# Waits on masks and layer norms themselves, and each value waited for once

## What is computed

```python
x = x + 0.5 * ffn0(layernorm(x))          # low rank: U1, V1, gelu, U2, V2
x = x + attn0(layernorm(x))               # 16 heads of 8, causal softmax, inner layer norm
x = x + 0.5 * ffn0(layernorm(x))
x = x + 0.5 * moe(layernorm(x))           # shared expert + top 2 of 8 experts
x = x + attn1(layernorm(x))               # causal, weight (second-order Taylor of exp), 16 heads
x = x + 0.5 * moe(layernorm(x))
```

## Time and profile before

| | us |
|---|---|
| median of three timed runs | 1515.85 (1515.03 to 1517.44) |
| profiled execution, its own time | 1510.05 |
| its span, first to last instruction | 1508.2 |
| TensorE matmul busy | 1238.7 (82%) |
| VectorE busy | 1078.3 (71%) |
| ScalarE busy | 750.7 (50%) |
| GpSimd busy | 308.1 (20%) |
| mean granted TensorE clock | 0.945 |

### The profile page before, as it was taken

How to read it: one execution, slowest core, us unless ns; L and a number is a source line. 1 busy time by engine, 2 the same in 40 slices (tenths; PEclk the granted TensorE clock), 3 DMA queues, 4 the chain that set the end, 5 groups by cost and what they waited for, 6 DMA issues and landing times. The chain is left out here.

```text
span 1508.2 us, 27324 instructions
## 1 busy us (share of the span) xinstructions
PE 1238.7 (82%) x10040; PEld 686.2 (45%) x10064; DVE 1078.3 (71%) x3235; ACT 750.7 (50%) x1246; POOL 308.1 (20%) x807
## 2 busy tenths in 40 slices
PE   5698659987798887888789877898778888898886
PEld 2354235444443454434454344544455345553544
DVE  6985368667886678866778658876687767866756
ACT  3166336652466425664276533765337653454442
POOL 1024001331014200242002420133101331122220
PEclk9699669999999989999889998999989999999999
DMA  3100000100010000100001000010000100101000
GB/s 115 43 2 1 7 22 15 29 8 22 8 33 12 8 22 8 43 2 10 27 1 43 8 10 20 1 43 8 21 9 3 42 1 5 46 1 43 2 1 14
DMA packets 37205, 28.77 MB, mean 19 GB/s; under 512 B 7961, under 2 KB 36305, under 8 KB 37073
## 3 DMA queue, kind: packets, MB, share of 16 engines
q1 hardware_dynamic: 37072, 27.04, 6.7%
HBM read 5.90 MB, written 2.10 MB: 5 GB/s over the span
## 5 line engine op out<-in xcount | busy, mean ns | idle before, releaser
L772 ACT ACTIVATE left<-bank 128x512 f32<-128x512 f32 x280 | 159.8, 600 | 84.3 <-PE bank L1242 81.4
L962 DVE TENSOR_REDUCE left<-bank 128x4 f32<-128x512 f32 x280 | 184.5, 683 | 23.1 <-PE bank L1223 21.7
L814 ACT ACTIVATE right<-bank 128x512 f32<-128x512 f32 x280 | 158.4, 601 | 85.6 <-PE bank L1329 79.0
L1165 PE MATMUL bank<-right,pairs 128*128 128x512 f16 x588 | 160.9, 397 | 23.7 <-DVE right L1041 17.1
L1221 PE MATMUL bank<-left 128*128 128x512 f16 (+1 forms) x448 | 128.5, 336 | 59.8 <-DVE left L952 28.5
L1092 DVE TENSOR_SCALAR right<-right 128x1024 f32<-128x1024 f32 x168 | 105.5, 654 | 62.0 <-ACT right L814 61.4
L1062 DVE SCALAR_TENSOR_TENSOR right<-bank,right 128x128 f32<-128x128 f32 x448 | 126.1, 344 | 30.6 <-PE bank L1305 23.9
L1355 PE MATMUL bank<-right 128*32 128x256 f32 (+3 forms) x1792 | 133.1, 435 | 0.0
L1305 PE MATMUL bank<-ew,right 128*128 128x128 f32 x896 | 119.3, 278 | 9.8 <-ACT right L791 6.0
L1305 PEld LDWEIGHTS bank<-ew,right 128*128 128x128 f32 x896 | 113.4, 191 | 29.8 <-DVE right L1062 11.5
L684 POOL TENSOR_TENSOR spareB<-neghalf 1x1 f32<-1x1 f32 x192 | 47.7, 249 | 327.9 <-DVE right L1092 252.5
(11 more groups left out here) (280 smaller groups left out, 2287.4 us busy)
## 6 DMA issues: line engine op xcount, KB each, us to landing
right<-right SPq DMA_DIRECT2D x168, 64.0 KB, 2.1
left<-left SPq DMA_DIRECT2D x168, 32.0 KB, 1.9
left<-x_dram SPq DMA_DIRECT2D x7, 256.0 KB, 2.8
out_dram<-right SPq DMA_DIRECT2D x7, 256.0 KB, 2.3
left<-left SPq DMA_DIRECT2D x24, 64.0 KB, 2.1
right<-right SPq DMA_DIRECT2D x24, 32.0 KB, 1.9
wo<-wo_dram SPq DMA_DIRECT2D x1, 512.0 KB, 3.2
ew<-ew_dram SPq DMA_DIRECT2D x1, 512.0 KB, 4.6
```

Of the source, the lines that this page charges most:

```text
L772: act.activation(h.probs[:, g % 2, u * S:(u + 1) * S], ps[:, :], ACT.Exp).then_inc(h.act, 1)
L814: act.activation(h.wts[:, p % 2, u * S:(u + 1) * S], ps[:, :], ACT.Square, bias=1.0, scale=FEAT ** -0.5).then_inc(h.act, 1)
L962: dve.tensor_reduce(h.bmax[:, u * NT:(u + 1) * NT], ps[:, :].rearrange("p (b k) -> p b k", k=P), AX.X, ALU.max).then_inc(h.dve, 1)
L1165: done = mm(out, left, right, start=first, stop=last)
```

## The change

`wait_apart`, the additions and the semaphore `carried` go; the masks' wait stands ahead of the first mask. The memset of one element goes from `Chain.then`, so that bn_aggr, max and the search for indices carry the wait on VectorE's own semaphore. A class `Passed` stands between the program and ScalarE's, VectorE's and TensorE's waits: it keeps the highest value that the engine has waited for on each semaphore and leaves out a wait for a value not above it. All `wait_ge`, `full` and `fill` of these three engines go through it; GpSimd's and SyncE's don't. The order lists and `LOOP` stay. Cut to its core:

```diff
-    def then(self, ins, carrier=None):
+    def then(self, ins):
         self.n += 1
         ins.then_inc(self.sem, 1)
         self.eng.wait_ge(self.sem, self.it * self.per + self.n)
-        if carrier is not None:
-            carrier()
...
+        class Passed:
+            def __init__(self, eng):
+                self.eng, self.seen = eng, {}
+
+            def wait_ge(self, sem, value):
+                if self.seen.get(sem.name, 0) < value:
+                    self.seen[sem.name] = value
+                    self.eng.wait_ge(sem, value)
...
-            for h in streams.values():
-                pool.tensor_tensor(h.spare[:, :], neghalf[0:1, 0:1], neghalf[0:1, 0:1], ALU.add).then_inc(h.carried, 1)
...
-            def wait_apart(h, it, n, sem, value):
-                pool.wait_ge(h.carried, it * h.carriers + n + 1)
-                pool.wait_ge(sem, value)
-                pool.tensor_tensor(h.spare[:, :], neghalf[0:1, 0:1], neghalf[0:1, 0:1], ALU.add).then_inc(h.carried, 1)
...
                 if u in COMPLETE0:
-                    wait_apart(h, it, g * NC + list(COMPLETE0).index(u), h.act, drained(h, it, step, "s"))
+                    pool.wait_ge(h.act, drained(h, it, step, "s"))
...
                     k = p * NC + list(COMPLETE1).index(u)
-                    wait_apart(h, it, k, h.plus1, it * NPAIR * NC + k + 1)
+                    pool.wait_ge(h.plus1, it * NPAIR * NC + k + 1)
...
-            def carrier():
-                dve.memset(spare_dve[:, :], 0.0)
...
-                h.chain.then(last, carrier)
+                h.chain.then(last)
...
-                pe.wait_ge(h.rrows_ready, it * 2 + p // GP + 1)
-                ps = fill(pe, h, it, step, "r")
+                passed.wait_ge(h.rrows_ready, it * 2 + p // GP + 1)
+                ps = fill(passed, h, it, step, "r")
```

More of the change, by code:

```diff
@@ L444, in attention_stream @@
             new = h.region.take
-            h.T, h.per, h.lns, h.carriers = TA, PERA, 4, NC * NG
+            h.T, h.per, h.lns = TA, PERA, 4
             h.ring, h.pv = h.banks[0:3], h.banks[3]
@@ L475, in taylor_stream @@
             new = h.region.take
-            h.T, h.per, h.lns, h.carriers = TB, PERB, 3, NC * NPAIR
+            h.T, h.per, h.lns = TB, PERB, 3
             h.ring, h.num, h.dsums = h.banks[0:2], h.banks[2], h.banks[3]
@@ L722, in norm @@
             def norm(h, it, k, step):
-                ps = full(act, h, it, step, "lnT")
+                ps = full(passed, h, it, step, "lnT")
                 if h in (A1, A2) and k == 2:
@@ L739, in down0 @@
                 if n % 2 == 0:
-                    ps = full(act, h, it, step, "mix")
+                    ps = full(passed, h, it, step, "mix")
                     act.activation(h.mixed[:, :], ps[:, :], ACT.Copy).then_inc(h.act, 1)
@@ L745, in up0 @@
                     f = int(unit[2:])
-                    ps = full(act, h, it, step, unit)
+                    ps = full(passed, h, it, step, unit)
                     act.activation(h.hid0[:, f, :], ps[:, :], ACT.Gelu_apprx_tanh, bias=b1[:, f:f + 1],
@@ L761, in shift @@
             def shift(h, it, g, step):
-                ps = full(act, h, it, step, "mT")
+                ps = full(passed, h, it, step, "mT")
                 act.activation(h.offs[:, g, :], ps[0:GH, :], ACT.Copy, scale=-1.0 / OFF_UNIT).then_inc(h.act, 1)
@@ L780, in gate @@
             def gate(h, it, n, step):
-                ps = full(act, h, it, step, "gate")
+                ps = full(passed, h, it, step, "gate")
                 act.activation(h.sgm[:, n % NS, :], ps[:, :], ACT.Sigmoid, scale=1 / W_SCALE)\
@@ L904, in down0 @@
                         tables_once()
-                    full(dve, h, it, f"norm {(0, 3)[n // 2]}", "lnT")
+                    full(passed, h, it, f"norm {(0, 3)[n // 2]}", "lnT")
                     h.chain.then(dve.tensor_tensor(h.ln[:, :, :], h.x[:, :, :], b2h[:, :, :], ALU.add))
                     return
-                ps = full(dve, h, it, step, "y")
+                ps = full(passed, h, it, step, "y")
                 first = h is A1 and isinstance(it, int) and it == 0
@@ L960, in rowmax @@
                     h.chain.start(it, chained(FRONT))
-                ps = full(dve, h, it, step, "s")
+                ps = full(passed, h, it, step, "s")
                 dve.tensor_reduce(h.bmax[:, u * NT:(u + 1) * NT], ps[:, :].rearrange("p (b k) -> p b k", k=P),
@@ L1011, in route @@
                 c = h.chain
-                dve.wait_ge(h.act, drained(h, it, f"router {n}", "router"))
-                c.then(dve.tensor_tensor(h.sel[:, :, :], h.s8[:, :, :], rbias[:, :, :], ALU.add), carrier)
+                passed.wait_ge(h.act, drained(h, it, f"router {n}", "router"))
+                c.then(dve.tensor_tensor(h.sel[:, :, :], h.s8[:, :, :], rbias[:, :, :], ALU.add))
                 for t in range(NT):
                     last = dve.max(h.top[:, t, :], h.sel[:, t, :])
-                c.then(last, carrier)
+                c.then(last)
                 for t in range(NT):
@@ L1049, in expert @@
                 if e == 0:
-                    dve.wait_ge(h.moe_out, first + 1)
+                    passed.wait_ge(h.moe_out, first + 1)
                     dve.scalar_tensor_tensor(out=h.acc[:, :, :].rearrange("p t d -> p (t d)"), in0=h.num[:, :],
@@ L1264, in out0 @@
             def out0(h, it, n, step):
-                pe.wait_ge(h.act, drained(h, it, "norm 2", "lnT"))
-                ps = fill(pe, h, it, step, "y")
+                passed.wait_ge(h.act, drained(h, it, "norm 2", "lnT"))
+                ps = fill(passed, h, it, step, "y")
                 for t in range(NT):
@@ L1300, in expert @@
                 else:
-                    pe.wait_ge(h.moe_added, first + e)
-                pe.wait_ge(h.act, drained(h, it, *unit_of_expert(n, e)))
+                    passed.wait_ge(h.moe_added, first + e)
+                passed.wait_ge(h.act, drained(h, it, *unit_of_expert(n, e)))
                 ps = (h.dsums, h.num)[e % 2]
@@ L1349, in num @@
                 if p:
[L1350 removed]
+                    passed.wait_ge(h.num_read, it * NPAIR + p)
                 for kt in (0, 1, 3, 2):
@@ L1368, in out1 @@
                 some = OUT1_PAIRS[n]
-                ps = fill(pe, h, it, step, "y")
+                ps = fill(passed, h, it, step, "y")
                 for p in some:
-                    pe.wait_ge(h.dve, drained(h, it, f"scale {p}", "r"))
+                    passed.wait_ge(h.dve, drained(h, it, f"scale {p}", "r"))
                     for t in range(NT):
```

236 lines of the change are left out of this document (118 added, 118 removed).

## The result

The changed kernel takes 1499.62 us in the median of 7 runs (1498.10 to 1502.16), the kernel before, on the same chip and between them, 1515.85 us (7 runs, 1506.00 to 1517.44): a ratio of 0.9903, interval 0.9881 to 0.9926. The change does what it says and more than three times what its own steps were held to be worth.

The account below looks back on a forecast made before the run. Hand-overs between engines were taken to bound the kernel; 0.35 + 0.19 + 0.08 = 0.62 us a turn, 5.0 us in eight turns, less 0.5, gave 4.5 us won: 1511.3 us, range 1504.5 to 1518.0.

Parts of the forecast that it names:

- What bounds the kernel, and where to look: Whole kernel: hand-overs between engines set the time; TensorE's matmuls wait 5.6 us for masks, 46.0 us for layer-norm centring.
- The mask's start: GpSimd's masks without the add: 0.20 us earlier where GpSimd waits, 0.15 us less where it works off masks.
- The term of 0.35 us a turn: Earlier masks on GpSimd at two places of a turn: 0.05 us ahead of L1253, 0.30 ahead of L1342.
- some 3: Sign in the profile after: the 5.6 us that L1342's matmuls waited for masks fall to some 3.
- The memsets of VectorE: Carriers before VectorE's bn_aggr and max: 0.03 us saved each on the path, 0.19 us a turn.
- Waits told once: Repeated waits dropped on TensorE, ScalarE, VectorE: 0.06 us in `scale` plus 0.02 elsewhere, 0.08 us a turn.
- What speaks against it: VectorE and GpSimd hold each other up; without the add at 676.69, where VectorE got in, three masks run on end.
- rival B: Masks on end hold VectorE, 0.36 us per lost hand-over; three a turn give +4.6 us, 1520.5; chance 0.12.
- The sum: All parts together: 0.62 us a turn, 5.0 us in eight turns, less 0.5 us: 4.5 us won.
- The forecast's times-eight: One turn of the loop was costed and multiplied by eight, the whole run holding eight times a turn's operations.
- The range and chances: 1504.5 to 1518.0 us; faster by over 0.2% 0.63, within 0.25, slower 0.12.
- C, the far gain: TensorE loads' other waits for masks count too: 4.4 us more won, 1506.9 us; chance 0.16.

Follow-up runs that it names:

- z6: Changed kernel with GpSimd's add back at four mask steps of stream B beside held VectorE operations, each mask there also waiting for its add: 1498.57 us.
- y1: Changed kernel, no adds, with three more long-met waits laid so that each mask's own value is asked for by a separate instruction: 1499.75 us.
- e2: Kernel before with only VectorE's memset carriers gone; GpSimd's adds and the repeated waits stay: 1518.40 us, ratio 1.0000.
- e3: Changed kernel with GpSimd's adds and VectorE's memsets put back, so only the repeated waits are left out: 1511.52 us, ratio 0.9960.
- e4: Changed kernel with GpSimd's adds in front of the masks put back, all else as changed: 1511.86 us, ratio 0.9963.
- z1: Changed kernel with GpSimd's add back at four of 24 mask steps of a stream B pass, beside held VectorE operations: 1506.00 us.
- x4: Kernel before with GpSimd's carriers as one-element memsets instead of adds: 1502.42 us, ratio 0.9901.
- z5: Kernel before with GpSimd's carriers as one-element copies instead of adds: 1517.40 us, ratio 0.9982.
- y5: Changed kernel with GpSimd's adds back in front of stream A's masks only (96 adds): 1500.59 us, ratio 0.9874.
- x1: Changed kernel with 576 more long-met wait instructions on GpSimd, laid ahead of the masks' own waits: 1498.45 us, ratio 0.9875.

## Why the prediction was wrong

*What bounds the kernel, and where to look.* Right in kind: hand-overs, and the two waits named, for masks and for centred values. The second was read as a matter of when the centring starts; its 46.0 us held VectorE's own stretched operations, and most of the gain that the rows show came from there (6.0 us), and 2.3 from the stretched `b2h`.

*The mask's start.* Right as durations, wrong as a price. A mask starts 0.08 us behind its value (0.09 said), and the row in front of the transposes is 0.28 us shorter (0.30 said). But z6 puts that lateness back and is as fast as the changed kernel, and y1 puts two thirds of the other back and costs 0.1 us. The term of 0.35 us a turn, 2.8 of 5.0 us, is nothing that these runs can measure. The matmuls' own waits for masks fell by 1.5 us (5.6 to 4.1), a little over half of the fall to "some 3" that was named.

*The memsets of VectorE.* 0.19 us a turn forecast, 1.5 us in all. e2 shows none (1.0000), with an interval that would hide it; VectorE's busy time moved by 0.2 us.

*Waits told once.* 0.08 us a turn forecast. The place itself did what was said: in the changed kernel's order of time the load of L1362 at 319.37 stands 0.05 us behind ScalarE's L813 (from 318.72, 0.60 long). The rows of three turns also give the turns' length, 180.6 and 180.2 us against 181.8 in the earlier trace rows:

```profile
319.37 0.10 PEld L1362 LDWEIGHTS bank<-right,spread 128*128 128x128 bf16 x1 [0.35 <-ACT right L813]
...
499.95 0.10 PEld L1362 LDWEIGHTS bank<-right,spread 128*128 128x128 bf16 x1 [0.34 <-ACT right L813]
...
680.17 0.10 PEld L1362 LDWEIGHTS bank<-right,spread 128*128 128x128 bf16 x1 [0.34 <-ACT right L813]
```

But the term was mis-sized while the adds stand: 0.4% (e3) instead of 0.04%. Why is open. The run medians of granted clock are 0.942 for e3 and e4 and 0.937 for the kernel before, which took 1524.28 us at 0.926 and 1512.81 at 0.949 in that job, some 5 us for 0.01: so by these two about 2.5 of e3's 6.3 us go with the clock, and neither what moves the clock nor the rest was tried.

*What speaks against it, and rival B.* Here is the step that failed. The row at 647.72 was read as "masks on end hold VectorE", and from the stretched add at 676.69 it was concluded that without the adds VectorE would be held longer. What was left out is the add at the front of each row:

```profile
647.58 0.18 POOL L684 TENSOR_TENSOR spareA<-neghalf 1x1 f32<-1x1 f32 x1
...
675.77 0.23 POOL L684 TENSOR_TENSOR spareB<-neghalf 1x1 f32<-1x1 f32 x1 [3.69 <-DVE right L1092]
```

In both places the operation of VectorE began while this add ran (647.69 and 675.87), and it stayed out over the masks behind it. Where VectorE comes while a mask runs it gets in behind that mask (0.84 us in the changed kernel). The add at 676.69 did let VectorE in, as was read: z1, which has the first add of this row and not the second, is held over three masks there. But that matters only as long as the first add stands, and the change takes away both. B said that L885, L1082, L1092 and L906 would grow; their longest fell from 1.20, 0.99, 1.80 and 1.39 us to 0.44, 0.79, 0.85 and 0.89. The rule of the Trainium skill (SBUF — State Buffer, § SBUF: two separate sides), that whoever starts first has the shared ports for one whole instruction, was set aside on the strength of the row at 647.72. By that rule VectorE should have got in behind the add. It didn't, so the rule doesn't cover that row, and I let that speak against it everywhere. In the changed kernel the rows follow it: no operation of L1089 lasts over more than the mask it met (850 ns at most). The same section says that a VectorE operation with two SBUF inputs, as `b2h`'s addition is, contends only with a GpSimd operation that reads SBUF. x4 against z5 fits that (0.89 against 1.38 us), but doesn't single it out, as said there.

*The sum.* Lengths of VectorE's operations were taken as given, so no term stood for their getting shorter: it was put at nothing. From the rows, two places alone are 5.2 us. The forecast's times-eight doesn't hold for these two, which stand once in each of the body's five turns. The three waits shown above fell by 9.8 us between the two profiled executions; e4 puts the adds at 12.2 (9 by the ratios); and from there to the kernel before lies e3's unexplained 0.4%.

*The range and chances.* C, the far gain, was given 0.16 and 1506.9 us. It came nearest by luck, for another cause, and was still 7 us short. No rival said that the adds themselves lengthen VectorE's operations. Priced from the three places where before's trace shows them longer, it would have been 0.47 + 0.56 + 0.29 = 1.3 us a turn more, some 6.5 us in five turns.

## What to carry to other kernels

Where GpSimd and VectorE run side by side, a tiny operation of GpSimd that only carries a wait is not free: here, where it read SBUF and masks followed it with nothing to wait for, a VectorE operation that began beside it could stay out over all of them. Put the wait on the work itself, or make the carrier a memset, or let GpSimd wait for the carrier before it goes on. Look for it where another engine waits behind the held operation; elsewhere it cost next to nothing (y5). And when a row of a trace shows a stretched operation, ask which instruction ran at the moment it began before saying what held it: here it was the short first neighbour that made the difference, not the long ones behind.

## What the runs showed of the hardware

- A one-element add or copy on GpSimd, followed by masks without a wait, stretches VectorE's 128x1024 operation from 0.69 to as much as 1.80 us (copy 1.74); with a memset in the same place the longest is 0.97, where the mask waits for its add 0.87, with nothing in front 0.85.
- How many masks the hold lasts over varies: one or all three at one and the same step (z1, 0.56 and 1.28 us), and what decides is open.
- Two masks on end let VectorE in between (0.84 us), and the second mask of 0.63 us then ends 0.45 later.
- 576 more wait instructions on GpSimd whose values are long there cost nothing (x1, 1498.45 us).
- Seven one-element memsets on VectorE, 0.059 us each by their rows, take 0.14 us together: such rows overlap and must not be multiplied.
- The kernel before scatters over 18 us in one job, its variants without held operations over 2 to 5 us.
